# A graph kernel on one core: another order of VectorE's work, with other ring sizes

## The reference, cut to what matters

```python
h = relu(layernorm(x))                       # 6250 nodes x 128
H = gelu(h @ W1.T + b1)
X_src = H[src]                               # 200000 edges, sorted by dst
W_tar = gelu(X_src @ WA.T) @ WB.T            # 4 mix weights per edge
cross = X_src[:, :, None] * W_tar[:, None, :]
agg = gelu(segment_sum(cross, dst))          # per node 128 x 4
out_edge = einsum('ehm,em->eh', agg[dst], W_tar)
agg_node = segment_sum(out_edge, dst) / maximum(cnt, 1)[:, None]
out = gelu(concatenate([agg_node, H], 1)) @ W2.T + b2
return x + out
```

## Time and profile before

| | us |
|---|---|
| median of 3 runs | 1254.35 |
| lowest, highest | 1250.93, 1255.43 |
| span of the profiled execution | 1435.7 |

### The profile page before, as it was taken

One profiled execution on the slowest core, in us unless ns is written; L12 is line 12 of the kernel. 1 busy time (PEld: TensorE's weight loads), 2 busy tenths in 40 slices (PEclk: granted clock), 3 DMA queues, 4 the chain that ended last, 5 costly groups with the idle time before them and its releaser, 6 DMA issues.

```text
span 1435.7 us, 26415 instructions
## 1 busy us (share of the span) xinstructions
PE 1168.7 (81%) x7416; PEld 773.5 (54%) x7416; DVE 915.1 (64%) x2876; ACT 635.0 (44%) x1498; POOL 849.4 (59%) x910
## 2 busy tenths in 40 slices
PE   5948777688887888988788888777888878779888
PEld 3724333366665555656556556555556655456544
DVE  8569987746764677675567767466666755262256
ACT  6976656344342455453455555244554531000023
POOL 5457655556566666666656566655655666656526
PEclk9965555589999999899989999988888999889978
DMA  6345544466555445444545444444444446765523
GB/s 203 130 135 175 171 145 161 142 184 180 167 169 165 134 135 135 126 138 138 144 123 137 121 123 133 140 129 120 127 121 109 125 127 185 176 186 169 174 47 84
DMA packets 100422, 205.73 MB, mean 143 GB/s; under 512 B 29570, under 2 KB 48336, under 8 KB 99611
## 3 DMA queue, kind: packets, MB, share of 16 engines
q1 hardware_dynamic: 74804, 146.92, 33.9%
q0 software_dynamic: 25472, 57.11, 16.2%
HBM read 171.73 MB, written 32.22 MB: 142 GB/s over the span
## 4 chain that ended last, share of the span: by engine, by line
PE 56%; DVE 15%; issue 14%; another core or an unknown queue 5%; DVEq 4%; ACT 3%; POOL 2%; DMA 2%; SPq 0%; ACTq 0%; POOLq 0%
PE ps L1565 23%; PE ps L1546 12%; PE ps L1518 12%; PE ps L1521 3%; DVE big L1195 3%; DVE big L1325 3%; DVE mask L1170 2%; PE ps L1570 2%; DVE q L1204 2%; DVEq L1152 2%; DVE big L1182 2%; POOL q L778 1%; DMA q<-node_table,src_g 1%; PE ps L1614 1%
## 5 line engine op out<-in xcount | busy, mean ns | idle before, releaser
L778 POOL DMA_INDIRECT q<-node_table,src_g x796 | 778.1, 977 | 497.1 <-PE ps L1521 218.6
L1565 PE MATMUL ps<-big,q 128*128 128x298 bf16 (+2 forms) x2940 | 522.7, 319 | 21.1 <-issue 14.2
L894 ACT ACTIVATE hot_b<-iota_b,q 128x128 bf16<-128x128 bf16 x848 | 270.0, 389 | 420.3 <-PE ps L1546 329.4
L1518 PE MATMUL ps<-mask,q 128*128 128x96 f32 x1592 | 291.2, 311 | 107.0 <-DVE mask L1170 67.8
L1565 PEld LDWEIGHTS ps<-big,q 128*128 128x128 bf16 x2940 | 286.5, 105 | 123.7 <-issue 31.1
L1195 DVE TENSOR_TENSOR big<-big,ps 128x294 f32 (+2 forms) x411 | 226.5, 551 | 186.4 <-PE ps L1546 125.6
L1518 PEld LDWEIGHTS ps<-mask,q 128*128 128x128 f32 x1592 | 244.9, 216 | 184.7 <-DVE mask L1170 118.3
L1546 PE MATMUL ps<-q,hot_b 128*128 128x294 bf16 (+2 forms) x848 | 221.7, 349 | 101.0 <-issue 58.4
L1204 DVE TENSOR_SCALAR q<-iota_a,q 128x294 bf16<-128x294 f16 (+2 forms) x848 | 238.0, 324 | 35.4 <-issue 19.8
L1170 DVE TENSOR_TENSOR mask<-eq,q 128x192 f32<-128x192 bf16 x398 | 141.9, 357 | 74.5 <-issue 40.0
L1182 DVE TENSOR_TENSOR big<-big,ps 128x120 f32 x398 | 110.2, 277 | 123.2 <-remote 53.0
(11 more groups left out here) (145 smaller groups left out, 665.7 us busy)
## 6 DMA issues: line engine op xcount, KB each, us to landing
q<-product_parts SPq DMA_DIRECT2D x245, 388.0 KB
product_parts<-big SPq DMA_DIRECT2D x24, 776.0 KB
q<-node_table,src_g POOLq DMA_INDIRECT x796
node_table<-big SPq DMA_DIRECT2D x12, 280.0 KB, 3.0
big<-node_table SPq DMA_DIRECT2D x24, 140.0 KB
own_part<-big SPq DMA_DIRECT2D x12, 256.0 KB, 3.0
out_dram<-q SPq DMA_DIRECT2D x12, 256.0 KB, 2.0
big<-own_part SPq DMA_DIRECT2D x2, 1024.0 KB, 6.2
```

What stands on the lines that cost most here:

```text
L778: pool.indirect_dma_start(out=ring[:, t % R, :], out_offset=None, in_=table, in_offset=bass.IndirectOffsetOnAxis(ap=src_g[:, t:t + 1], axi ...
L894: last = nc.scalar.activation(hot_b[:, b % 2, i, :], iota_b[:, :], ACT.Abs, bias=nkey_b[:, t:t + 1])
L1518: nc.tensor.matmul(o[:, 0:MIX * W], ring[:, s + t, 0:D], mask[:, b, t, :, :], start=(t == 0), stop=(t == G - 1))
L1565: last = nc.tensor.matmul(ps[:, 3 + m, 0:n], c[:, LEAD + P * (MIX * part + m):LEAD + P * (MIX * part + m + 1)], counts[k % 2][:, a, c0:c1] ...
```

## The change

VectorE's loop over the slots is written anew. Before the loop the masks and one-hots of the first slot are made. Then, in slot i: masks of slot i + 1; additions of this slot's gathered pairs (`pending_g`); one-hots of slot i + 1; additions of all of this slot's counts. The special work of a slot keeps its place before or behind that. The other engines' code stays as it is, but for the sizes: R from 10 to 12, HA from 6 to 8, CB from 4 to 3, and eight registers each for the column numbers.

```diff
--- before.py
+++ after.py
@@ -53,7 +53,7 @@
 TG = G1 - G0
 NG = TG // G
 NA = N - D0 + W
-R = 10
+R = 12
 ROW = 140
 TP = 2 * (D + MIX)
 NP = 1 + SPL * MIX
@@ -66,11 +66,11 @@
 EV_BANK = [2, 4, 5, 6]
 MB = 4
 EB = 6
-HA = 6
+HA = 8
 HB = 4
 LEAD = 16
 CROW = LEAD + SPL * MIX * D
-CB = 4
+CB = 3
 AB = 7
 NAB = NT // AB
 WROWS = MIX * SPL
@@ -215,7 +215,7 @@
         dn = at(0, MIX * D0).rearrange("p (m n) -> p m n", m=MIX)
 
         assert MIX * D0 <= HALF and NT * D <= ACC0 - HALF
-        QW = 3104 + R * ROW + CTT + -(-CTT // 2) + HA * NT * CW // 2 + MIX * SW
+        QW = CB * CROW // 2 + R * ROW + CTT + -(-CTT // 2) + HA * NT * CW // 2 + MIX * SW
         q = sb("q", [P, QW])
         cbuf = q[:, 0:CB * CROW // 2].bitcast(bf16).rearrange("p (b x) -> p b x", b=CB)
         RING0 = CB * CROW // 2
@@ -1144,8 +1144,8 @@
             v.wait_ge(early_zeroed, 1)
             v.wait_ge(consts, 7)
 
-            regs_g = [nc.vector.alloc_register(f"start_g{i}") for i in range(6)]
-            regs_c = [nc.vector.alloc_register(f"start_c{i}") for i in range(4)]
+            regs_g = [nc.vector.alloc_register(f"start_g{i}") for i in range(8)]
+            regs_c = [nc.vector.alloc_register(f"start_c{i}") for i in range(8)]
             starts_g, starts_c = {}, {}
 
             def column(reg, cell, largest):
@@ -1272,9 +1272,27 @@
                 v.wait_ge(sums_checked, S - 1)
                 link(nc.vector.tensor_reduce(marks[:, 5:6], smax[:, 2:K], axis=AX.X, op=ALU.max))
 
+            def prepare_gathers(slot):
+                for g in slot.gathers:
+                    starts_g[g] = column(regs_g[g % 8], base_g[:, g:g + 1], N - D0)
+                    if g % 2 == 1 and g + 1 < NG:
+                        make_eq(g + 1)
+                    make_mask(g)
+
+            def prepare_counts(slot):
+                for c in slot.counts:
+                    if c.index == 0:
+                        v.wait_ge(keys_ready, KEYED[c.chunk])
+                    cell = GROUP0[c.chunk] + c.index
+                    starts_c[c.number] = column(regs_c[c.number % 8], base_c[:, cell:cell + 1],
+                                                WIDE[c.chunk] - CWS[c.chunk])
+                    hots(c)
+
             make_eq(0)
-            pending_g, pending_c = [], None
-            for slot in SLOTS:
+            pending_g = []
+            prepare_gathers(SLOTS[0])
+            prepare_counts(SLOTS[0])
+            for i, slot in enumerate(SLOTS):
                 s = slot.stage
                 if (s, slot.at - KEY_LAG) in KEY_AT:
                     k = KEY_AT[s, slot.at - KEY_LAG]
@@ -1286,33 +1304,24 @@
                     nc.vector.tensor_reduce(smax[:, b:b + 1], sstage[0:1, 0:WIDE[b]], axis=AX.X, op=ALU.max)\
                         .then_inc(sums_checked, 1)
                 if s == S and slot.at % 2 == 0 and slot.at // 2 < NAB:
-                    i = slot.at // 2
+                    b = slot.at // 2
                     v.wait_ge(counts_added, CGG)
-                    nc.vector.tensor_reduce(most_p[:, i:i + 1], counts[1][:, AB * i:AB * i + AB, :], axis=AX.XY,
+                    nc.vector.tensor_reduce(most_p[:, b:b + 1], counts[1][:, AB * b:AB * b + AB, :], axis=AX.XY,
                                             op=ALU.max).then_inc(most_ready, 1)
                 if s == S and slot.at == 2 * NAB:
                     v.wait_ge(most_ready, NAB)
                     nc.vector.tensor_reduce(most_p[:, NAB:NAB + 1], most_p[:, 0:NAB], axis=AX.X, op=ALU.max)\
                         .then_inc(most_ready, 1)
-                for g in slot.gathers:
-                    starts_g[g] = column(regs_g[g % 6], base_g[:, g:g + 1], N - D0)
-                    if g % 2 == 1 and g + 1 < NG:
-                        make_eq(g + 1)
-                    make_mask(g)
-                    pending_g.append(g)
-                    if g % 2 == 1 and g >= 3:
-                        add_group(pending_g.pop(0))
-                        add_group(pending_g.pop(0))
+                if i + 1 < len(SLOTS):
+                    prepare_gathers(SLOTS[i + 1])
+                pending_g += slot.gathers
+                while len(pending_g) >= 2:
+                    add_group(pending_g.pop(0))
+                    add_group(pending_g.pop(0))
+                if i + 1 < len(SLOTS):
+                    prepare_counts(SLOTS[i + 1])
                 for c in slot.counts:
-                    if c.index == 0:
-                        v.wait_ge(keys_ready, KEYED[c.chunk])
-                    cell = GROUP0[c.chunk] + c.index
-                    starts_c[c.number] = column(regs_c[c.number % 4], base_c[:, cell:cell + 1],
-                                                WIDE[c.chunk] - CWS[c.chunk])
-                    hots(c)
-                    if pending_c:
-                        add_counts(pending_c)
-                    pending_c = c
+                    add_counts(c)
                 if s == 0 and slot.at % 2 == 0:
                     h = slot.at // 2
                     v.wait_ge(row_loaded[h % 2], 16 * (h // 2 + 1))
@@ -1334,9 +1343,6 @@
                                             cf[:, h % FBUFS, 0:pair_size(h), :, :].rearrange("p a m d -> p a (m d)"),
                                             c3[:, h % PBUFS, 0:pair_size(h), LEAD + MIX * D:LEAD + 2 * MIX * D],
                                             ALU.subtract).then_inc(part_lo, 1)
-                if not slot.counts and pending_c:
-                    add_counts(pending_c)
-                    pending_c = None
                 if s == S and slot.at == 20:
                     v.wait_ge(early_sums_loaded, 16)
                     make_weights(sums_e, parts_e, early_weights_ready, link, chained)
```

## The result

| | before | after |
|---|---|---|
| median of the runs, us | 1253.96 (1250.93 to 1255.43) | 1311.53 (1311.15 to 1317.35) |
| ratio | | 1.048, 95% interval 1.0443 to 1.0518 |
| span of the profiled execution, us | 1435.7, 1251.0 in a second trace | 1309.8 |

A forecast was written before the change was run, and what follows sets the result against it. No engine was taken as saturated: TensorE, VectorE and GpSimd wait for one another through the order. Gains 5 + 10 + 19 + 25 + 3 + 6 - 3 = 65 us, scaled to 57, gave a forecast of 1198 us, range 1150 to 1262.

The forecast's parts named there:

- "The rest is what a better order can win", 178 us: Stages 1 to 5: time in which TensorE is not busy, 178 us together, taken as what a better order can win.
- The scaling by 0.874: Whole kernel: gains summed in profiled time (1435.7 us) are multiplied by 0.874 to give unprofiled time (1254.35 us).
- Two-count slots, 19 and 25 us: Most of stages 2 and 3: VectorE goes round without waiting for TensorE's counts, gaining 19 and 25 us.
- Three-count slots, 3 us: Mainly stage 4: third count group held 2.0 to 2.6 us a slot, replacing 50 us idle; gain taken as 3 us.
- slower rival: Three-count slots: 3.5 us hold each, stage 4 clock falling to 0.80 (20 us more), 1285 us in all; chance 0.18.
- Stage 0, 5 us: Stage 0: of VectorE's 30 us not busy, mostly register loads, a gain of 5 us.
- Stage 1, 10 us: Stage 1: masks a slot ahead cover the places where VectorE computes keys, a gain of 10 us.
- Stage 5, 6 us: Stage 5: bounds check loses 2, the larger gather ring gains 2.5, earlier masks gain 6; 6 us taken.
- The rings, -3 us: Ring sizes: three part buffers instead of four delay loads behind seven large ones in stage 5, a loss of 3 us.
- The range: Whole kernel: 1150 to 1262 us, said to leave out the slower rival's upper part, some 0.15.

The follow-up runs named there:

- e4: Changed kernel with one-hots and count additions back in the old alternating order, masks and group additions kept in the new: 1527.49 us, ratio 1.222.
- e15: Changed kernel, but in three-count slots the first count group is added before the next slot's one-hots: 1261.20 us, ratio 1.0078, on a faster-kind chip.
- e3: Changed kernel with one exchange: VectorE adds this slot's counts before making the next slot's one-hots: 1259.17 us, ratio 1.005.
- e8: The changed kernel unchanged, timed again on a chip of the slower kind: 1466.57 us beside 1440.71 of before, ratio 1.0201.
- e2: Kernel before in its old order, with only the changed ring sizes (gathers 12, one-hots 8, part buffers 3): 1245.79 us, ratio 0.9945.
- e16: Stages 0 to 3 in the order of e3, stages 4 and 5 in the order of before, rings of after: 1234.95 us, ratio 0.986, faster-kind chip.

## Why the prediction was wrong

**"The rest is what a better order can win", 178 us.** This step failed first. TensorE's idle time in the earlier trace rows was taken as waits made by the order. In the second trace, with the same order, it is 79 us in the same five stages. Of the difference of 99, the rows with "issue" as cause make nearly all: 119 us in the first trace (18.9 of the 39.6 in the earlier trace rows), 17 in the second. The name of the cause alone would not have told this, for e4's 236.7 us of "issue" are made by the order; the comparison of the two traces does. On the chips of the timed result stages 2 to 4 last 193, 201 and 198 us, near the floors of 190 to 198 that the prediction itself worked out for VectorE and GpSimd. The estimate of VectorE's need in stage 4, 195 us against 189 measured, was near; it was the room above it that wasn't there.

**The scaling by 0.874.** A trace 14% longer than the timed runs was scaled instead of doubted. No factor turns one kind of run into the other: stage 0 and the tail have the same length in both traces (192 and 58 us), stages 1 to 4 are 19 to 28% longer in the first (158 for 133, 231 for 193, 245 for 201, 253 for 198 us), stage 5 is 12% longer (203 for 181).

**Two-count slots, 19 and 25 us.** Measured +1 and +12 in stages 2 and 3 here, and +2 and 0 on the slower kind, where 23.6 of the 35 us and 23.3 of the 40 that the prediction counted as room have "issue" as cause. Of the 12, 6 go when only the four three-count slots are changed (207 us in e15), and all when counts are added first in every slot (199 us in e3), so additions behind one-hots cost something in two-count slots too.

**Three-count slots, 3 us.** This term makes the loss: -62 measured. The hold itself was forecast well: 2.0 to 2.6 us a slot and 50 us in the stage, measured 2.3 on average (3.48 at most) and 57 us idle. What failed is that these 50 us were to take the place of 50 us of other idle time. On the chips of the result there were only 21 to replace, so 36 us came on top. On the slower kind there were 49, 26.5 of them with "issue" as cause, and after has 75 (e8), stage 4 being 27 us longer. The other 26 us are the clock, 0.84 instead of 1.00, which the sum had at 0.88 on both sides. The slower rival put it at 0.80 and 20 us, and that part came true on the chips of the result; its hold of 3.5 us in every three-count slot did not. The Trainium skill, TensorE: Matmul & The Clock Gate, "A second HAM failure mode: psum-queue depth-cycling", says that short idles between groups of matmuls bring the half clock back. The rows agree: the stage with a pause in half its slots is the one that lost the clock, 1.00 to 0.84, and with shorter waits before counts, 35.2 us in e3 and 33.5 in e15 where after has 50.2, it came back to 0.94 and 0.96.

**Stage 0, 5 us.** Right, and too small: 10 us. TensorE is busy 131.48 us instead of 143.65 there, at a clock of 0.55 instead of 0.50; its waits for masks stay, 37.8 us instead of 35.1. (The stage has 76 count groups, one a tile, and not 64 as the description of the kernel says.)

**Stage 1, 10 us.** 5 measured. TensorE's wait for the first load of parts is longer, 6.6 us where the second trace of before has 3.2 and e2, with the same three buffers, 2.9; stage 0 ends sooner here:

```profile
PE ps L1571 <- DMA q<-product_parts: 6.6, 1, 6.6
```

**Stage 5, 6 us.** 1 measured. Waits for gathers stay, 62.6 us in before and 43.5 in after, with hardly any effect on the end:

```profile
DVE mask L1170 <- DMA q<-node_table,src_g: 62.6, 38, 6.4
```

```profile
DVE mask L1170 <- DMA q<-node_table,src_g: 43.5, 25, 6.6
```

**The rings, -3 us.** With the wrong sign: together they win 7 us (e2), and there and in after no product waits for its parts outside the start of stage 1.

**The range.** 1150 to 1262 left out what happened, for which "slower" stood at 0.19 with 1285. Its clock term came true, its longer hold did not, and stage 4's idle time grew by 36 us, about its 34, only because it started lower. It set them against 25 us of gains in the other stages; measured are 15, and 13 more lost in stages 2 and 3.

## What to carry to other kernels

When a profiled execution is much longer than the timed runs (here 14%), ask where the difference lies before anything is scaled, and take another trace; idle time without a releaser may be the chip's, as in the first trace, or the order's, as in e4, and only a second trace or an experiment tells which. A wait that a change adds need not take the place of idle time that is there: here 36 of 57 us came on top. Working a step ahead decouples two engines only as far as there are buffers for what comes back: with two banks for counts, a third group a slot made the order serial again. Where the engines already wait little for one another, as in stage 4, another order can add waits and hardly remove any; the gain was in stages 0 and 1, so a change of order is best made stage by stage, as e16 did.

## What the runs showed of the hardware

The kernel before took 1252 to 1254 us on two chips and on that of the result, and 1441 to 1456 on three others, the runs of one chip within about 1% of one another (4 to 19 runs each). Instructions last equally long in both traces (a 298-column product matmul at full clock 0.29 us, a gather issue 0.95). In the trace that is like the slower kind TensorE pauses, at times inside a run of matmuls that wait for nothing (0.89 and 0.43 us in the unit shown), and the one signal followed above came 4.1 us late. The cause was not found. It was not tried to provoke the pauses. A change can weigh differently by kind: after is 4.8% slower on one and 2.0% on the other, the mixed order 1.4% faster and 0 to 0.4%.
